# RWKV-6 block with a ternary FFN on 8 cores: all weight loads of the main loop issued by GpSimd's queue instead of SP's

## What is computed

```python
def _rwkv6(x, ...):
    x_prev = concat([zeros, x[:, :-1]])
    xr, xk, xv, xw = (tm_i * x + (1 - tm_i) * x_prev for i in r, k, v, w)
    r = sigmoid(xr @ W_r.T); k = xk @ W_k.T; v = xv @ W_v.T
    w = -softplus(-(xw @ W_w.T)) - 0.0001
    # 16 heads of 64; per token: o = r @ (s + exp(u + k) v^T);  s = exp(w) s + k v^T
    o = layernorm_per_head(o) * ln_w + ln_b
    return (o * r) @ W_o.T

def _ffn(x):                       # bitlinear: row-wise int8 activations, ternary weights
    gate = silu(_bitlinear(x, w_gate)); up = _bitlinear(x, w_up)
    return _bitlinear(gate * up, w_down)        # 1024 -> 4096 -> 1024

x = x + _rwkv6(_layernorm(x)); x = x + _ffn(_layernorm(x))
```

## Time and profile before

| | us |
|---|---|
| timed runs: median of 2 (lowest, highest) | 13372.16 (13359.11, 13385.2) |
| profiled execution, its own time | 13359.85 |
| its span, slowest core (core 2) | 13358.3 |
| spans of the 8 cores | 13271.8 to 13358.3 |
| busy: TensorE, VectorE, ScalarE, POOL | 2810.9, 4326.6, 2276.2, 170.7 |
| mean granted TensorE clock, share of full speed | 0.717 |

### The profile page before, as it was taken

The page is one execution under the profiler, slowest core; times in us unless marked ns, Lnnn a source line. Parts: engine busy times, 40 slices in busy tenths (PEclk is TensorE's granted clock), DMA queues, the critical chain, the costliest instruction groups (busy, mean ns, idle before and its releaser), DMA issues.

```text
span 13358.3 us, 44639 instructions; the slowest of 8 cores (13271.8 to 13358.3 us)
## 1 busy us (share of the span) xinstructions
PE 2810.9 (21%) x14044; PEld 1151.3 (9%) x14220; DVE 4326.6 (32%) x3858; ACT 2276.2 (17%) x2088; POOL 170.7 (1%) x60
## 2 busy tenths in 40 slices
PE   0000000002231322232222313231324132413232
PEld 0000000001010111011011101110111011101110
DVE  0010100103335334433533262417241724172426
ACT  0001011113210311031112111211221022102210
POOL 0000000000000000000000000000000000000000
PEclk9999999997665666556665666575657565756575
DMA  2222222321011101101110111011101010111011
GB/s 51 53 70 50 75 48 49 96 63 38 22 47 37 36 28 41 50 22 35 38 60 10 41 33 58 11 47 28 57 12 52 24 57 17 57 25 44 22 50 32
DMA packets 942364, 563.83 MB, mean 42 GB/s; under 512 B 617008, under 2 KB 879536, under 8 KB 942128
## 3 DMA queue, kind: packets, MB, share of 16 engines
q1 hardware_dynamic: 936368, 550.47, 14.5%
q0 software_dynamic: 5760, 10.49, 0.5%
HBM read 424.21 MB, written 52.43 MB: 36 GB/s over the span
## 4 chain that ended last, share of the span: by engine, by line
DVE 29%; SPq 19%; PE 18%; ACT 15%; DMA 13%; issue 4%; DVEq 2%; POOL 1%; ACTq 0%; POOLq 0%
DVE arn L1378 7%; SPq L384 6%; PE ps L1280 5%; DMA arnb<-wqtu 4%; PE ps L1287 4%; DVE arn L1376 4%; SPq L238 3%; ACT L1300 2%; PE ps L1426 2%; SPq L494 2%; SPq L1398 2%; SPq L801 2%; DMA arnb<-arnb 2%; PE ps L576 2%; DVE arn L1224 2%
## 5 line engine op out<-in xcount | busy, mean ns | idle before, releaser
L1280 PE MATMUL ps<-arnb 128*128 128x512 bf16 x2000 | 668.2, 489 | 2315.6 <-DMA arnb<-wqtu 1719.5
L1426 PE MATMUL ps<-arnb 128*128 128x512 bf16 x2008 | 537.5, 432 | 2626.6 <-DMA arnb<-arnb 1714.7
L1310 DVE SCALAR_TENSOR_TENSOR arn<-ps,arn 128x512 f32<-128x512 f32 x256 | 192.2, 751 | 2413.2 <-ACT arn L1300 2413.2
L1378 DVE TENSOR_TENSOR arn<-arn 128x2048 f32<-128x2048 f32 x384 | 880.1, 2292 | 29.6 <-issue 1.3
L1300 ACT ACT_TABLE_LOAD x256 | 328.4, 1283 | 2228.8 <-PE ps L1287 2228.8
L370 DVE SCALAR_TENSOR_TENSOR arnb<-arn,thr,arnb 128x1024 bf16<-128x1024 f32 (+1 forms) x72 | 118.1, 1640 | 1713.2 <-ACT arnb L358 1713.2
L576 PE MATMUL ps<-arnb 128*128 128x512 bf16 x1505 | 390.7, 406 | 1305.9 <-DMA arnb<-wtr 1208.7
L354 ACT ACT_TABLE_LOAD x72 | 92.4, 1283 | 2665.3 <-DVEq L327 1120.6
L1287 PE MATMUL ps<-arnb 128*128 128x512 bf16 x2016 | 538.1, 412 | 2.9 <-issue 1.5
L297 PE MATMUL ps<-cpool_s,arn 128*1 128x1 f32 x6 | 0.6, 164 | 2452.6 <-DVE arn L291 2452.6
L1376 DVE TENSOR_SCALAR arn<-arn 128x2048 f32<-128x2048 f32 x384 | 471.2, 1227 | 30.0 <-issue 0.9
(11 more groups left out here) (163 smaller groups left out, 6041.3 us busy)
## 6 DMA issues: line engine op xcount, KB each, us to landing
arnb<-wqtg SPq DMA_DIRECT2D x64, 1024.0 KB, 5.5
arnb<-wqtu SPq DMA_DIRECT2D x64, 1024.0 KB, 8.0
arnb<-wqtd SPq DMA_DIRECT2D x64, 1024.0 KB, 9.7
arnb<-arnb SPq DMA_TRANSPOSE x2880, 2.3
arn<-wg SPq DMA_DIRECT2D x256, 128.0 KB, 2.7
arn<-wu SPq DMA_DIRECT2D x256, 128.0 KB, 2.7
arn<-wd SPq DMA_DIRECT2D x64, 512.0 KB, 6.5
arn<-x SPq DMA_DIRECT2D x8, 2048.0 KB, 7.7
```

The lines of the kernel that those rows point to most:

```text
L1280: t.matmul(ps[:, bg * 512:(bg + 1) * 512], bass.AP(AR16.tensor, 2 * O_B6 + kc * 512 + g * 128, [[PIT16, 128], [1, 128]]), bass.AP(AR16.ten ...
L1378: v.tensor_add(YF, YF, BF)
L1426: m = t.matmul(ps[:, b * 512:(b + 1) * 512], bass.AP(AR16.tensor, 2 * GT[g] + kc * 128, [[PIT16, 128], [1, 128]]), bass.AP(AR16.tensor, 2 ...
```

## The change

All loads by `wload` in the main loop move from SP's queue to POOL's: `wtr`, `wtk`, `wtv`, `wtw`, `wto`, the pairs `wqtg` and `wqtu`, and both halves of `wqtd`. Sizes, buffers and what each waits for stay as they were, except that the waits are now POOL's. The transposes, the x load and the output store stay on SP. The pieces that matter:

```diff
-                    P.wait(sy, "sy", "pe")
-                    P.wait(sy, "sy", "q1", ffnw_q1)
-                    wload(sy, 2 * O_WWIN, 1024, wtr_h, 0, D, 8, 1024, "qwr")
-                    P.wait(sy, "sy", "qxl")
-                    P.wait(sy, "sy", "qgqt")
-                    wload(sy, 2 * O_B1, 1024, wtk_h, 0, D, 4, 1024, "qwk")
-                    wload(sy, 2 * O_B8, 1024, wtk_h, 512 * D, D, 4, 1024, "qwk")
+                xlq = P.cnt["qxl"]
+
+                @blk.gpsimd
+                def _(gp, xlq=xlq):
+                    P.wait(gp, "gp", "pe")
+                    P.wait(gp, "gp", "q1", ffnw_q1)
+                    wload(gp, 2 * O_WWIN, 1024, wtr_h, 0, D, 8, 1024, "qwr")
+                    P.wait(gp, "gp", "qxl", xlq)
+                    P.wait(gp, "gp", "qgqt")
+                    wload(gp, 2 * O_B1, 1024, wtk_h, 0, D, 4, 1024, "qwk")
+                    wload(gp, 2 * O_B8, 1024, wtk_h, 512 * D, D, 4, 1024, "qwk")
...
-                    @blk.sync
-                    def _(sy, fc=fc, wgo=wgo, wuo=wuo, qwin=qwin):
-                        P.wait(sy, "sy", "q1", ffnw_q1)
+                    @blk.gpsimd
+                    def _(gp, fc=fc, wgo=wgo, wuo=wuo, qwin=qwin):
+                        P.wait(gp, "gp", "q1", ffnw_q1)
                         if fc > 0:
-                            P.wait(sy, "sy", "v")
-                        P.wait(sy, "sy", "pe")
-                        wload(sy, 2 * wgo, 512, wqtg_h, fc * 512, FF, 8, 512,
+                            P.wait(gp, "gp", "v")
+                        P.wait(gp, "gp", "pe")
+                        wload(gp, 2 * wgo, 512, wqtg_h, fc * 512, FF, 8, 512,
                               qwin)
-                        wload(sy, 2 * wuo, 512, wqtu_h, fc * 512, FF, 8, 512,
+                        wload(gp, 2 * wuo, 512, wqtu_h, fc * 512, FF, 8, 512,
                               qwin)
...
-                @blk.sync
-                def _(sy):
-                    P.wait(sy, "sy", "pe")
+                @blk.gpsimd
+                def _(gp):
+                    P.wait(gp, "gp", "pe")
                     for qr in range(NG):
-                        wload(sy, 2 * WDQ[qr], 512, wqtd_h, qr * 1024 * D,
+                        wload(gp, 2 * WDQ[qr], 512, wqtd_h, qr * 1024 * D,
                               D, 8, 512, "qwd", pieces=1)
```

More of the change, by code:

```diff
@@ L601, in build @@
                                    extra_pe_wait=("qwr", wr_q1))
-                @blk.sync
-                def _(sy):
-                    P.wait(sy, "sy", "pe")
-                    wload(sy, 2 * O_WWIN, 1024, wtv_h, 0, D, 8, 1024, "qwv")
+                @blk.gpsimd
+                def _(gp):
+                    P.wait(gp, "gp", "pe")
+                    wload(gp, 2 * O_WWIN, 1024, wtv_h, 0, D, 8, 1024, "qwv")
                 wv_q1 = P.cnt["qwv"]
@@ L611, in build, with _ @@
                                    extra_pe_wait=("qwk", wk_q1))
-                @blk.sync
-                def _(sy):
-                    P.wait(sy, "sy", "pe")
-                    wload(sy, 2 * O_B1, 1024, wtw_h, 0, D, 4, 1024, "qww")
-                    wload(sy, 2 * O_B8, 1024, wtw_h, 512 * D, D, 4, 1024, "qww")
+                @blk.gpsimd
+                def _(gp):
+                    P.wait(gp, "gp", "pe")
+                    wload(gp, 2 * O_B1, 1024, wtw_h, 0, D, 4, 1024, "qww")
+                    wload(gp, 2 * O_B8, 1024, wtw_h, 512 * D, D, 4, 1024, "qww")
                 ww_q1 = P.cnt["qww"]
@@ L967, in build, with _ @@
                     stup_m[c] = P.cnt["v"]
[L969 to L972, removed]
+                @blk.gpsimd
+                def _(gp):
+                    P.wait(gp, "gp", "pe")
+                    wload(gp, 2 * O_B1, 1024, wto_h, 0, D, 8, 1024, "qwo")
                 wo_q1 = P.cnt["qwo"]
@@ L1408, in build, with _ @@
                     else:
-                        @blk.sync
-                        def _(sy):
-                            P.wait(sy, "sy", "pe")
+                        @blk.gpsimd
+                        def _(gp):
+                            P.wait(gp, "gp", "pe")
                             for qr in range(NG):
-                                wload(sy, 2 * WDQ[qr], 512, wqtd_h,
+                                wload(gp, 2 * WDQ[qr], 512, wqtd_h,
                                       qr * 1024 * D + 512, D, 8, 512, "qwd")
```

## The result

The changed kernel takes 13266.81 us (median of 9 runs, 13253.11 to 13273.57), the kernel before 13376.49 us (8 runs). The ratio is 0.992 with a 95% interval of 0.991 to 0.9931: about 110 us or 0.8% faster, clear of the noise, and inside 2%. The profiled execution took 13255.64 us against 13359.85, its slowest core spans 13254.0 us.

A forecast was written before the change was run, and what follows sets the result against it. No engine was full; a chain of handoffs was taken to bound the kernel. From 13360 us the terms -198 - 11 + 28 + 129 + 18 = -34 gave 13326 us, with a range of 13170 to 13600 us.

The forecast's parts named there:

- likeliest case: Whole kernel: POOL takes 1.2 to 3.0 us per load and the early fc=0 gain comes whole; 13326 us, chance 0.42.
- G: Time POOL takes to issue one moved weight load: 0.56 us if fixed, 4.5 if by runs, taken as 2.5.
- rival 1: POOL's issue of loads is nearly free (0.56 to 1.2 us each): 13176 to 13204 us, taken as 13190; chance 0.22.
- A: First FFN column block (fc=0) of each tile: its weights load early, saving 24.8 us per tile, 198 us in all.
- Rival 3: At fc=0 something holds group 0's L1310, so only the load's own 8.9 us is saved: 13453 us, chance 0.05.
- B: Projection start: `wtr` is loaded early, no longer behind 32 transposes on SP, saving 1.4 us per tile, 11 in all.
- C: Tile boundary: early `wtr` shares bandwidth with the output store and x load, costing 3.5 us per tile, 28 in all.
- D: The 56 exposed FFN weight pairs, now issued by POOL: each 2.3 us longer, 129 us in all; bounds 22 and 300.
- E: Second half of `wqtd`, exposed at the FFN's end, now issued by POOL: 2.3 us longer each, 18 us in all.
- F: First half of `wqtd`, issued by POOL well before its need: costed at nothing, up to 48 us if VectorE must wait.
- rival 4: POOL and VectorE shut each other out around 5190 to 5205 us in the trace: 13374 us, no change; chance 0.04.
- Rival 2: POOL's issue time goes by runs and the FFN loop pays: slower, 13541 us at 4.5 us per load; chance 0.27.

## Why the prediction was right or wrong

The direction and the range held: 13326 was forecast, 0.3% faster, and 0.8% was measured, inside 2% as was thought likeliest. That the time lies in the likeliest case's own range (13243 to 13358) is in part luck. That case asked for G between 1.2 and 3.0, and G is 0.88, in the premise of rival 1. What POOL's late start and the store cost above the working brought the time back up. By its steps:

- **A was right.** 24.8 us per tile were forecast, 25.6 measured in the mean, 22.7 to 24.8 us being left of 48.0 to 49.9; the run with this part alone has nearly the same 205 us. The 9.6 us for g=1 as the first group after a long idle time did not come: in the second tile it took 8.2, so that g=1 to g=3 took 21.6 us and not 24.5. TensorE's wait names the transpose, ScalarE and VectorE let g=0 through as the order of their queues said. Rival 3 is out.
- **B was right**: 11 forecast, 7.8 measured. The loads of `wtk`, `wtv`, `wtw` and `wto`, costed at nothing, cost nothing: the rest of the tiles changed by -1.0 us.
- **C was right in mechanism, and near in size by two errors that cancel**: 28 forecast, 32.5 measured. The forecast took 3.5 us 8 times, but there are 7 boundaries; each costs 4.6 us, within the bounds of 0 and 5.2. The run with `wtr` behind the x load takes it away, the run on one queue shows that it doesn't take a second queue. The weak point was the change's and not the forecast's: 8 us were bought with 32.
- **D is the step that failed in size**: 129 forecast, 77 measured. The term G was taken at the middle of its ends, 2.5 us, and is 0.88, close to the fixed cost of 0.56 in the earlier trace rows. The step then had a second error the other way: with G = 0.88 its working gives 0.68 us per pair, 38 in all. Measured is 1.14 us in the mean gap before L1284 (8.89 to 10.03), 64 in all. The working counted from the issue and left out the time from the release to the issue, and there POOL starts late: 0.68 us in the mean, 0.13 on SP (4910.25 to 4910.38). So the landing, 9.8 us after the release, fell between the 10.7 of the forecast and the 8.8 of rival 1. The last 13 us of the 77 are in TensorE's matmuls (18.3 to 18.5 us per block). That POOL's path causes them is not shown: with the pairs on SP they took 18.3 to 18.5 us too, and in the two other runs with a gap of 10 us 18.3 and 18.4.
- **E** follows D: 18 forecast, 6.2 measured, 5 by the working with G = 0.88. The near match hides two parts: TensorE's wait for the load grew by 9.0 us over the 8 tiles (15.1 to 16.3 each), and the work behind it was 2.7 us shorter.
- **F and rival 4**: no cost, as forecast. The reason given (they don't meet) is right for this kernel; which of the two would give way was open, and the run with the load under VectorE's work shows that it is POOL.
- **Rival 1** held in its premise, generation nearly free, and not in its time: 13190 against 13256 of the profiled run. It took C at nothing or little, and D at 22. With all terms as forecast but G = 0.88 the sum is 13360 - 198 - 11 + 28 + 38 + 5 = 13222.
- **Rival 2** is out: it needs more than 3.0 us for each load of 1 MB, and 0.88 was measured.

The two rules weighed: the Trainium skill, "DMA: Bandwidth & Descriptors", section "Anatomy of one DMA — SWDGE (gpsimd) path", says that many descriptors can be emitted before the cost shows; the runs agree in essence, with 0.537 us for 128 runs, 0.75 for 512 and 0.88 for 1024, which is a fixed half microsecond and 0.4 ns a run between the ends (the 512 runs are of 2 KB and lie above that line). The Trainium skill, "SBUF — State Buffer", section "SBUF: two separate sides", says that VectorE's two-port modes lock GpSimd out: the trace agrees with 1.27 and 1.93 us instead of 0.88, if the fast op is in such a mode, which no row names. It lets either side block the other; here only VectorE blocked POOL, and the fast op never exceeded 1.231 us on any core.

## What to carry to other kernels

When a load sits behind other work on an in-order queue, first ask whether it could stand ahead of it on the same queue: here the two loads of fc=0 moved forward on SP bring 1.5%, and moving every load to another queue brings 0.8%. Move to the slower path only loads that are hidden, and keep an early load off the transfers that stand on the chain (one wait more was worth some 32 us). And look at what a load waits for before asking who issues it: the same loads released one block earlier brought 4.3% on top of the 1.5%, seven times the 0.6% that POOL's path cost while they were exposed.

## What the runs showed of the hardware that I had not expected

- From a release to the start of its DMA instruction POOL takes 0.60 to 0.89 us at the exposed pairs of the changed kernel, SP 0.13 in the kernel before.
- The same 2 MB go in 544 packets from POOL and in 2080 from SP (the 13 us windows around an exposed pair), at much the same rate once they flow, 302 to 416 GB/s from POOL and 340 to 391 from SP: the larger packets of about four runs did not move data faster.
- Where TensorE waits longer before a block, its matmuls tend to take longer: 17.1 us per block of 4 groups with no gap, 18.3 to 18.5 with gaps of 8.9 or 10.0 us, 19.8 with 11.9. The granted clock, over the whole blocks and all cores, goes with it: 0.90 in the run with loads ahead on SP, 0.80 in the kernel before and in the changed one, 0.745 with 16 pieces. In the second tile of the changed kernel it fell to 0.5 (1.2 GHz) at 4878.7, 2.2 us after the last product of fc=0, while TensorE waited for its load; the first 8 matmuls of fc=1, from 4886.6, took 3.57 us at that level, and the 8 from 4863.28, at the full 2.4 GHz, 1.89.
